# Attention's front: VectorE splits Q and K of the first eight heads before the second sequence's norm, GpSimd splits those of the other eight

## What is computed

```python
xn = layer_norm(x, norm_w, norm_b)
q = (xn @ q_w + q_b).reshape(Bx, Tx, H, -1)        # Bx = 2, Tx = 1024, H = 16
k = (xn @ k_w + k_b).reshape(Bx, Tx, H, -1)
att = jnp.einsum('bnhl,bmhl->bnmh', q, k)
att = att + (1.0 - mask) * -1000000.0
att = jax.nn.softmax(att, axis=2)
v = ((xn @ v_w + v_b) * src_mask[:, :, None]).reshape(Bx, Tx, H, -1)
y = jnp.einsum('bnmh,bmhl->bnhl', att, v).reshape(Bx, Tx, Dx)
...
h = layer_norm(y, sb_norm_w, sb_norm_b) * (1.0 + scale) + shift
h = jax.nn.silu(h) @ out_w + out_b
return x + h
```

## Time and profile before

| what | us |
|---|---|
| median of 3 runs | 2041.7 (2038.73 to 2043.12) |
| the profiled execution, time | 2041.11 |
| its span | 2039.4 |
| PE busy | 1908.9 (94%) |
| DVE busy | 1601.1 (79%) |
| ACT busy | 1415.8 (69%) |
| POOL busy | 1043.8 (51%) |

### The profile page before, as it was taken

One profiled execution on the slowest core, in us unless ns is written; L12 is line 12 of the kernel. 1 busy time (PEld: TensorE's weight loads), 2 busy tenths in 40 slices (PEclk: granted clock), 3 DMA queues, 4 the chain that ended last, 5 costly groups with the idle time before them and its releaser, 6 DMA issues. The chain is left out here.

```text
span 2039.4 us, 32415 instructions
## 1 busy us (share of the span) xinstructions
PE 1908.9 (94%) x12312; PEld 1342.6 (66%) x12312; DVE 1601.1 (79%) x2109; ACT 1415.8 (69%) x2410; POOL 1043.8 (51%) x603
## 2 busy tenths in 40 slices
PE   6979999999998999989999999999988999998997
PEld 3654999759995799689974998699843222222323
DVE  5555899659994899689985998799968777777642
ACT  3416999379972999699927996998642566665665
POOL 3021799309992499469930998299725100002000
PEclk9989899989999999999999999999988999999999
DMA  5031211111211121011100111111101111111000
GB/s 193 1 129 47 68 58 58 47 39 54 58 48 53 32 58 58 23 42 58 56 13 12 57 57 45 43 58 58 32 20 40 33 33 33 33 33 33 10 22 21
DMA packets 57546, 95.18 MB, mean 47 GB/s; under 512 B 14951, under 2 KB 23559, under 8 KB 55982
## 3 DMA queue, kind: packets, MB, share of 16 engines
q1 hardware_dynamic: 55854, 88.90, 14.5%
q0 software_dynamic: 1536, 4.20, 0.7%
HBM read 73.55 MB, written 6.91 MB: 39 GB/s over the span
## 5 line engine op out<-in xcount | busy, mean ns | idle before, releaser
L966 POOL TENSOR_TENSOR A<-A 128x1024 f32<-128x1024 f32 x384 | 895.7, 2398 | 300.3 <-ACT small L878 141.1
L886 ACT ACTIVATE A<-A,negA 128x512 f32<-128x512 f32 x768 | 549.2, 717 | 30.2 <-DVE A L947 23.6
L947 DVE TENSOR_TENSOR_SCAN A<-A,small,PS 128x512 f32<-128x512 f32 x384 | 453.8, 1258 | 8.0 <-ACT A L886 4.9
L947 DVE TENSOR_TENSOR_SCAN A<-A,PS 128x512 f32<-128x512 f32 x384 | 431.8, 1198 | 22.4 <-PE PS L799 10.9
L824 PE MATMUL PS<-ident,A 128*128 128x128 f32 x3072 | 402.8, 274 | 13.0 <-POOL A L966 9.6
L1480 DVE TENSOR_REDUCE A<-PS 128x1 f32<-128x512 f32 x512 | 324.7, 682 | 100.2 <-PE PS L1467 98.8
L799 PE MATMUL PS<-A 128*128 128x128 f32 x3072 | 385.0, 277 | 0.2
L1714 ACT ACTIVATE A<-PS 128x1024 f32<-128x1024 f32 x256 | 260.0, 1023 | 180.3 <-PE PS L1678 176.4
L799 PEld LDWEIGHTS PS<-A 128*128 128x128 f32 x3072 | 364.1, 193 | 3.9 <-DVE A L947 0.9
L824 PEld LDWEIGHTS PS<-ident,A 128*128 128x128 f32 x3072 | 348.8, 142 | 20.2 <-POOL A L966 12.5
L863 ACT ACTIVATE A<-A,small 128x512 f32<-128x512 f32 x320 | 229.3, 717 | 14.5 <-PE PS L805 14.5
(11 more groups left out here) (192 smaller groups left out, 1838.3 us busy)
## 6 DMA issues: line engine op xcount, KB each, us to landing
A<-scrc SPq DMA_DIRECT2D x192, 256.0 KB, 3.1
A<-A SPq DMA_DIRECT2D x360, 32.0 KB
scr<-A SPq DMA_DIRECT2D x4, 1024.0 KB, 4.9
W<-in_wa SPq DMA_DIRECT2D x2, 1536.0 KB, 9.7
X<-in_x SPq DMA_DIRECT2D x4, 512.0 KB, 5.3
scr<-W SPq DMA_DIRECT2D x128, 1.5 KB
out<-X SPq DMA_DIRECT2D x4, 512.0 KB, 2.9
W<-in_w SPq DMA_DIRECT2D x1, 1984.0 KB, 7.6
```

Of the source, the lines that this page charges most:

```text
L886: e.activation(A_B[i % 4], r.DT[:, dt, ci * 512:(ci + 1) * 512], ACT.Exp, scale=negA[:, r.n, dt * 16 + s:dt * 16 + s + 1]).then_inc(*decay ...
L947: e.tensor_tensor_scan(h, a, u, init, ALU.mult, ALU.add).then_inc(*scanned.up((q, i)))
L966: e.tensor_tensor(h, h, CB[k % 2].unsqueeze(1).broadcast_to([128, 2, 512]), ALU.mult).then_inc(*weighed.up((q, pair)))
```

## The change

Two places change. `on_pool` now gives GpSimd both Q and K of heads 8 to 15 of the first sequence, so one split (three instructions) moves from VectorE to GpSimd. And on VectorE the splits that stay with it, those of heads 0 to 7 of the first sequence, now stand ahead of the norm of the second sequence. No other engine's list changes.

```diff
         def on_pool(b, h, n):
-            return b == 1 or (h == 1 and n == 1)
+            return b == 1 or h == 1
...
             e.memset(MN, 0.0).then_inc(*dve.up())
-            norm3_v(e, w, 1)
             for job in front_jobs(0):
                 if not isinstance(job, int) and job[3] and job[4] and not on_pool(*job[0:3]):
                     rest_of_parts(e, w, job, dve)
+            norm3_v(e, w, 1)
             for i in range(LEAD):
                 ahead_v(e, w, i)
```

## The result

| | before | after |
|---|---|---|
| median of 14 runs, us | 2042.36 (2038.73 to 2047.56) | 2038.22 (2035.41 to 2042.05) |
| ratio, 95% interval | | 0.9982 (0.9974 to 0.9991) |
| profiled execution, us | 2041.11 | 2035.97 |
| its span, us | 2039.4 | 2034.2 |

By the ratio, the change makes the kernel faster by 3.7 us (1.8 to 5.3 by the interval; the two medians are 4.1 us apart). Forecast were 10.2 us and a time of 2031, with a range of 2027 to 2036; the median lies above it.

The account below looks back on a forecast made before the run. PE was taken to bound the kernel, with a hole before the last layer's first trial. 7.5 us of wait and 2.7 of clock made 10.2 us, so 2041.7 became 2031.5, forecast as 2031, range 2027 to 2036.

Parts of the forecast that it names:

- What bounds the kernel there: Last layer's beginning: PE, busy 94% of the span, stops 7.5 us before the first trial, waiting for head 0's stack DMA.
- Part 1: VectorE, splits ahead of the norm: 3.2 us each, so head 0's stack is ready at 1508.9, before PE ends turning.
- Part 2: Second sequence's norm behind the splits: ends at 1507.2, at most 1511.4; PE waits 0 for it, 0.5 us at most.
- Part 3: One more split on GpSimd: done between 1515.4 and 1518.6, in place of 1510.1; cost on the path 0.
- Part 4: PE goes straight from turning to the first trial: 7.5 us less wait, and 2.7 us less because the clock stays up.
- Part 5: Lead and steps behind it: the whole lead moves 10.2 us earlier and the gain arrives at the end.
- The allowance of 2 us for the low clock at the lead's end: Half-clock stretch, 1568 to 1588, expected 10 us earlier; 2 us either way if either end moved by 4 us.
- (a): Rival: the wait shrinks but the clock stays low, or the trial waits for something else; gain 3 to 7.5 us, chance 0.08.
- a PE wait at L243 for L217: Sign against the forecast: PE's turning of the second norm waits for VectorE's scaling.
- a low clock around 1515: Sign against the forecast: a stretch at granted clock 0.50 there, where 1.00 was expected from 1487 to about 1557.

Follow-up runs that it names:

- e4: Changed kernel with GpSimd's splits of sequence 0 cut in halves, same work in all; eight scalings 8.41 us for 11.60, ratio 0.9953 to the kernel before.
- e9: e1 with 12 short write-only GpSimd fills of 128x256 beside VectorE's eight scalings; all eight together lose 0.6 us.
- e1: Changed kernel with one more wait: GpSimd begins its two splits only after VectorE's last scaling of the norm; ratio 0.9957 to the kernel before.
- e7: e1 with two idle PE products per item in the lead's last 16 items, to hold the clock; ratio 0.9956 to the kernel before.
- e3: Kernel before with only the split moved to GpSimd, the norm still first on VectorE; ratio 1.0029 to the kernel before.

## Why the prediction was wrong, step by step

- **What bounds the kernel there**: right. The hole is gone as soon as head 0's splits stand first.
- **Part 1**, splits of 3.2 us each with GpSimd idle beside them: right. First split to the end of the second: 1491.25 to 1497.84. SP's first stack DMA starts at 1497.93 in the profile after, 12.3 us after the first Q product; 1499.5 - 1487.25 = 12.3 was predicted.
- **Part 2, the norm behind them: this is the step that failed.** It took 0 and had 0.5 us as the high end of what PE would wait; PE's turning took 4.5 us more than before. The high end for the scaling was 6.9 us, from a ratio of 2.6 between one subtraction beside GpSimd and one alone. It took 11.60. A ratio was the wrong form: the hold is a wait until GpSimd's current instruction ends, as e4 and the ends of the 35 held scalings show. In the earlier trace rows VectorE's subtraction is 1.92 us longer (3.15 for 1.23) because it waits for what is left of GpSimd's subtraction of 2.51 us. Read so, the same rows give the right price: eight scalings, each short, and six GpSimd instructions lined up beside them, so six waits of up to 2.2 us, and the norm ends with GpSimd's second split. From the power's end at 1504.6 that is 10.8 us later, 1515.4, in place of the 1511.4 taken as the upper bound. What rows 6 and 7 could not tell is that GpSimd gets in again between two scalings each time; that was seen only afterwards.
The rule weighed there was the Trainium skill's, "SBUF — State Buffer", section "Who interferes with whom": the first of a GpSimd instruction and a VectorE instruction in a two-port mode has the shared ports for the whole instruction, and the other is blocked in full. The trace agrees on the whole instruction: the scalings in the profile after and in e4 wait for its end, and in e9 for that of ones that only write. Which of the two counts as first is not settled by their starts in the records: the third and the sixth scaling of the profile after begin 13 ns ahead of GpSimd's subtraction and are held all the same. The prediction quoted the rule and then bounded it by the ratio, which is not what it says.
- **Part 3**, GpSimd's additional split costs the path nothing: right in what was asked (it ends at 1513.89, ahead of the next high part), wrong in that the question was too narrow. It asked who waits for GpSimd's result and not who stands beside it on VectorE.
- **Part 4**, 7.5 us of wait and 2.7 us of clock: right, once the hold is taken away. e1 has 7.7 and 2.5. In the changed kernel they are 3.2 and 1.4, since PE's new waits in the turning lowered the clock once more.
- **Part 5**, nothing gets lost between the lead and the steps: right. With e1 the whole 10.2 us stand at the first weighing. Of the way behind it the profiles say less: 9.4 us are left at the end in e1 and 3.6 of 4.6 in the changed kernel, and what takes the rest was not found. The allowance of 2 us for the low clock at the lead's end was too much; e7 has it at under 1 us in all.
- **The rivals.** Nearest came (a), which was given 0.08, with 3 to 7.5 us of gain and with the reason "a norm at its upper bound". Its reason was right, its mechanism only in part: the trial waits for nothing, PE waits at the turning, and 1.4 of the 2.7 us of clock do come back. Its chance was held down by the wrong bound, and the range to 2036 was too narrow for the same reason. Two of the signs named as "wrong would be" came as written: a PE wait at L243 for L217, and a low clock around 1515.

In numbers, at the first weighing of the profiles: 10.2 us predicted and reached in e1, 4.6 in the changed kernel. The 5.6 us between are 4.5 us of PE's waits and slow turning, and 1.1 us of slower items behind it.

## What to carry to other kernels

When work moves to GpSimd, look at what VectorE does at that moment and count instructions, not microseconds: a VectorE instruction that needs the shared way waits for the end of GpSimd's running one, so a series of short VectorE instructions beside long GpSimd ones goes on at GpSimd's pace, one for each of its instructions. If VectorE's result is urgent and GpSimd's is not, let GpSimd wait; a wait that holds back an early result cost nothing here and was worth 5 us. A short stop of the engine that bounds the kernel costs more than its length where its clock falls in it (by the profiles, 7.5 us of hole and 2.5 more behind it), while the same low clock where another engine sets the pace cost under 1 us in 20.

## What the runs showed of the hardware

- A tensor_scalar of 128x256 fp32 with one SBUF input and two per-partition scalars, 0.41 us alone, was held by each GpSimd instruction it met: 2.2 to 2.3 us beside subtractions of 2.13 us, 1.18 beside casts of 1.04, up to 1.32 beside halves (1.16 to 1.21), 0.47 beside fills of 0.34, 0.43 beside copies of 0.29. In all 35 cases it ended 0.14 to 0.15 us after the GpSimd instruction. GpSimd's own subtractions beside scalings were not longer than 2.17 us for 2.12.
- Batch-norm statistics (L206, 2.71 us for eight) and their folding (0.62) were not held beside the same GpSimd split.
- Not shown: whether a scaling in another form (with its accumulator written out, say, or from PSUM) would pass GpSimd unheld.
- Where VectorE's instructions were subtractions and casts of 128x1024 (e3), both paid: VectorE's cast 2.51 us for 0.70, GpSimd's second subtraction of a split 3.19 us for 2.12.
